# Zero products on TensorE behind two attentions and inside two layer norms, and the variances of all pairs ahead of the logits

## The reference

```python
h = jnp.concatenate([tokenise(x), txt], axis=1)                 # 8 x 269 x 64
h = h + L0_attn(_layernorm(h))       # Nystrom attention, 8 heads, 6 pseudo-inverse steps
h = h + L0_ffn(_layernorm(h))        # 8 experts, top 2, router on the normed stream
h = h + L1_attn(_layernorm(h))       # exp(-gamma * squared distance) attention, 8 heads
h = h + L1_ffn(_layernorm(h))        # shared MLP and 4 experts, top 2

def _L0_ffn_ref(x, Wr, br, ln_g, ln_b, W1, b1, W2, b2):
    logits = xt @ Wr + br
    top_p, top_idx = jax.lax.top_k(jax.nn.softmax(logits, axis=-1), TOP_K)
    ...
    xn = (xt - mu) * jax.lax.rsqrt(var + LN_EPS)
```

## Time and profile before

| what | value |
|---|---|
| median of 3 runs | 731.64 us (730.41 to 740.26) |
| the profiled execution | 736.04 us |
| its span | 734.2 us |
| mean granted clock of TensorE in it | 0.939 |
| TensorE busy | 681.5 us (93% of the span), 6033 products |
| weight loads | 527.5 us (72%) |
| VectorE, ScalarE, GpSimd busy | 413.5, 377.6 and 229.7 us |
| DMA | 8.23 MB, most of it in the first 40 us |

### The profile page before, as it was taken

The page is one execution under the profiler, slowest core; times in us unless marked ns, Lnnn a source line. Parts: engine busy times, 40 slices in busy tenths (PEclk is TensorE's granted clock), DMA queues, the critical chain, the costliest instruction groups (busy, mean ns, idle before and its releaser), DMA issues. The chain is left out here.

```text
span 734.2 us, 15178 instructions
## 1 busy us (share of the span) xinstructions
PE 681.5 (93%) x6033; PEld 527.5 (72%) x6033; DVE 413.5 (56%) x843; ACT 377.6 (51%) x1035; POOL 229.7 (31%) x204
## 2 busy tenths in 40 slices
PE   9887898999999999999889999869999999989896
PEld 5676798988989898988785555557666666647555
DVE  3457347667575767674525333426777777764322
ACT  4656447565655647473246555335555455544531
POOL 4155325343544344444300434023222222201001
PEclk9997699999999999999958999957999999996999
DMA  8200000000000000000000000000000000000000
GB/s 267 99 3 1 1 1 3 2 1 2 1 2 2 2 1 3 2 1 2 1 1 1 1 1 1 1 1 1 1 1 1 1 2 1 1 1 1 1 15 17
DMA packets 5214, 8.23 MB, mean 11 GB/s; under 512 B 3608, under 2 KB 4120, under 8 KB 4760
## 3 DMA queue, kind: packets, MB, share of 16 engines
q1 hardware_dynamic: 4552, 7.20, 3.1%
q10 hardware_dynamic: 592, 0.07, 0.1%
HBM read 6.71 MB, written 0.55 MB: 10 GB/s over the span
## 5 line engine op out<-in xcount | busy, mean ns | idle before, releaser
L977 POOL TENSOR_TENSOR STD<-STD,NN 91x492 f32<-91x492 f32 (+1 forms) x96 | 104.0, 1101 | 149.2 <-DVE NN L1106 78.7
L677 PE MATMUL PS<-ST 128*91 128x123 f32 x768 | 92.9, 272 | 4.8 <-DVE ST L1112 4.6
L1106 DVE SCALAR_TENSOR_TENSOR NN<-ST,PS 91x492 f32<-91x492 f32 x96 | 62.9, 661 | 56.3 <-PE PS L677 56.3
L677 PE MATMUL PS<-NN 128*91 128x123 f32 (+1 forms) x768 | 89.6, 268 | 3.2 <-DVE NN L1106 3.2
L677 PEld LDWEIGHTS PS<-ST 128*91 128x91 f32 x768 | 83.5, 159 | 11.0 <-DVE ST L1112 7.1
L677 PEld LDWEIGHTS PS<-NN 128*91 128x91 f32 x768 | 82.2, 160 | 10.4 <-DVE NN L1106 6.4
L1746 PE MATMUL PS<-QR,KA 128*128 128x270 f32 x256 | 72.2, 413 | 0.0
L895 ACT ACTIVATE STD<-ST 91x492 f32<-91x492 f32 (+1 forms) x96 | 51.6, 569 | 39.6 <-DVE ST L1112 39.6
L1860 DVE TENSOR_SCALAR CL<-PS,K 128x270 f32<-128x270 f32 x144 | 65.7, 496 | 9.8 <-PE PS L1746 4.5
L1112 DVE SCALAR_TENSOR_TENSOR ST<-PS,STD 91x492 f32<-91x492 f32 (+1 forms) x96 | 55.9, 599 | 22.1 <-POOL STD L977 12.4
L1801 ACT ACTIVATE EX<-CL,NG 128x540 f32<-128x540 f32 x64 | 46.7, 741 | 32.8 <-DVE CL L1860 32.7
(11 more groups left out here) (326 smaller groups left out, 1250.5 us busy)
## 6 DMA issues: line engine op xcount, KB each, us to landing
TP<-taps SPq DMA_DIRECT2D x1, 1204.0 KB, 16.1
MA<-mat SPq DMA_DIRECT2D x1, 1120.0 KB, 7.5
MF<-mat SPq DMA_DIRECT2D x1, 1024.0 KB, 12.6
WI<-wide SPq DMA_DIRECT2D x1, 902.0 KB, 9.0
CO<-const SPq DMA_DIRECT2D x1, 512.0 KB, 15.7
MQ<-mat SPq DMA_DIRECT2D x1, 512.0 KB, 16.4
out<-OS SPq DMA_DIRECT2D x8, 45.0 KB
XA<-xpatch SPq DMA_DIRECT2D x1, 256.0 KB, 2.8
```

Source lines behind the costliest of these rows:

```text
L677: last = nc.tensor.matmul(PS[0:NL, PINV + q, h % 4 * SW + c0:(h % 4 + 1) * SW], x[:, h, 0:NL], x[:, h, c0:SW], start=True, stop=True)
L977: nc.gpsimd.tensor_tensor(TD[:, 4 * q:4 * q + 4, c0:SW], SA[:, 4 * q:4 * q + 4, c0:SW], NN[0:NL, 4 * q:4 * q + 4, c0:SW], ALU.subtract).th ...
L1106: v.scalar_tensor_tensor(out=NN[0:NL, own, :], in0=ST[0:NL, b % 2, own, :], scalar=N_S, in1=heads4(PS[0:NL, PINV + q, 0:4 * SW]), op0=ALU. ...
```

## The change

ZK and spin move out of the token stage, so that all stages can use them, and spin can now also write only partitions low to 127, with 256 columns in fp32. The first attention gets two zero products ahead of its last output projection and 14 behind it, all into bank 2. The second attention gets 14 behind its last product, into bank 5, after a wait on VectorE's reads of that bank. In norm_pe the variances of all four pairs come first; then each pair has one zero product of 32 outputs (partitions 96 to 127 of bank VARS) ahead of its logits, and four such follow the last logits.

```diff
+        ZK = sb("ZK", [128, 512], F32R)
...
+        def spin(n, bank=7, low=0):
+
+            for _ in range(n):
+                if low:
+                    nc.tensor.matmul(PS[low:128, bank, 0:256], ZK[:, 0:128 - low].bitcast(F32), ZK[:, 0:256].bitcast(F32),
+                                     start=True, stop=True)
+                else:
+                    nc.tensor.matmul(PS[:, bank, :], ZK[:, 0:128], ZK[:, :], start=True, stop=True)
...
         SCORES, PROJ, PINV, TAIL = 0, 4, 4, 6
         SUMS, TOPS = 3, 1
+        SPARE = 2
...
                 attend(B - 1, 0)
                 attend(B - 1, 1)
+                spin(2, SPARE)
                 out_proj(B - 1)
+                spin(14, SPARE)
...
             for p in range(BP):
                 pe.wait_ge(sem(tag + "_squared"), p + 1)
                 variances(p, VARS, KT * p).then_inc(sem(tag + "_var"), 1)
+            for p in range(BP):
+                spin(1, VARS, 96)
                 pe.wait_ge(sem(tag + "_kept"), p + 1)
                 logits(p, weights, n).then_inc(sem(tag + "_logit"), 1)
+            spin(4, VARS, 96)
             for p in range(BP):
                 pe.wait_ge(sem(tag + "_widened"), p + 1)
...
                 batches(pe, body)
+                need(pe, ("d_vm", atb("d_vm", B // 2 - 1, 1, 4, 4)))
+                spin(14, 5)
```

More of the change, by code:

```diff
@@ L212, in program @@
         PL = ts("PL", [128, BP, NL - 1])
-        ZK = ts("ZK", [128, 512], F32R)
         HC = B * NI // 2
-        SPIN = 7
         assert HC == 256 and GRP == 3 and PAD % GRP == 1 and NI % GRP == 1 and (NX - 2) % GRP == 0
@@ L347, in _ @@
             def _(pe):
-                def spin(n):
-                    for _ in range(n):
-                        nc.tensor.matmul(PS[:, SPIN, :], ZK[:, 0:128], ZK[:, :], start=True, stop=True)
                 avp = CO[:, C_AVP:C_AVP + 128]
```

## The result

The changed kernel takes 739.51 us (median of 4 runs, 735.84 to 749.78), the kernel before 731.58 us beside it (4 runs, 730.41 to 740.26). The ratio is 1.0083, with an interval of 1.0046 to 1.0119: some 6 us longer (+3.4 to +8.7), where +0.7 was forecast. The ratio leaves out the slow one of the changed kernel's four runs, 749.78 us at a granted clock of 0.939 where the other three have 0.953 to 0.959, and so it gives a smaller difference than the two medians. The forecast's range of 725 to 742 us held the result, and it is within 2%. The profiled execution took 735.84 us with a span of 734.0 and a mean granted clock of 0.959; the one of before took 736.04 with 734.2 and 0.939. So the two profiles alone would say "no change, at a better clock", and the times say otherwise. That is the question of this study.

A forecast was written before the change was run, and what follows sets the result against it. TensorE, busy 93% of the span, was taken as the bound, its clock dipping in both norms. Held norms -3.9 us plus one fall +4.6 gave +0.7; 731.64 + 0.7 = 732.3 us, range 725 to 742.

The forecast's parts named there:

- The barriers: Behind each attention, 14 zero products make TensorE last at the barrier, delaying the centring by +2.4 and +2.5 us.
- The order in the norm with the clock held: In both norms at high clock, TensorE reaches the spreading 9.24 us after the centring's start, instead of 11.79 and 8.27.
- d: Norm before the first feed-forward, after the first attention; predicted -4.3 us with the clock held.
- h: Norm before the last feed-forward, after the second attention; predicted +0.4 us with the clock held.
- Does the clock hold: Likeliest, chance 0.40: it holds in one norm and falls in the other, a fall costing +4.6 us (+1.8 to +7.4).
- The base of the sum: Whole kernel: gains set against the profiled 736.04 us, then carried to the median, 4.4 us lower, giving 731.64.
- milestones: Gate weights' cast at 393.91 and turn at 683.50 us; work behind them was called the same and at full clock.
- B: Rival, chance 0.22: the clock falls in both norms, zero products run at half clock before the spreading; +5.3 us, 736.9.
- A: Rival, chance 0.25: the clock holds in both norms; -3.9 us, 727.7.
- C: Rival, chance 0.04: zero products with 32 outputs don't keep the clock up, low from the first logits; +14.4 us, 746.
- D: Rival, chance 0.05: the norm's zero products run beside the logits, saving 1.9 us per norm; A would be 723.9.
- The warned place: In the norm, reciprocals ready at 5.3 us, but logits and zero products cover the early variances' worth; 3.9 us slack.

The follow-up runs named there:

- e4: Changed kernel without the norms' eight zero products and with 4 instead of 14 behind each attention; 0.9906 of the kernel before, median 726.04 us.
- e1: Changed kernel with the old norm order and no zero products in the norm, keeping 2, 14 and 14 around the attentions; 1.0112 of the kernel before.
- b2: The kernel before, unaltered, profiled a third time; a single execution of 734.26 us.
- e2: Changed kernel without the zero products around the attentions, only the norm's edit kept; 1.0176 of the kernel before.
- e7: Kernel before with only the variances of all pairs moved ahead of the logits, no zero products added; 0.9943 of the kernel before.
- e10: Changed kernel with the norm's eight zero products as fp32r, 128 outputs, 512 columns, into bank 5; 1.0161 of the kernel before.
- e6: Changed kernel with the old norm order, no zero products in the norm, and 2, 4 and 4 around the attentions; 1.0029 of the kernel before.

## Why the prediction was nearly right, and where it was not

**The barriers: right.** 2.83 became 5.18 (+2.35 for +2.4 predicted), 2.47 became 4.93 (+2.46 for +2.5). The barrier did wait for TensorE's queue. The two zero products ahead of the projection cost nothing, as said: the projection starts 0.05 us behind ScalarE's copy.

**The order in the norm with the clock held: the right mechanism, one term mis-sized.** The spreading was to come 9.24 us behind the centring and came at 10.21 in both profiles of d. Of the missing 1.0 us 0.8 are in the alternation: a zero product and the logits of one pair take 0.55 (372.59 to 373.14) and 0.58 us (373.14 to 373.72) in turn, where I had 0.45 and 0.48. The rest is in the centring (1.90 for 1.80) and the last four zero products (1.85 for 1.80). Rows of one form confirm the prediction's prices, 0.46 for the last four zero products and 0.48 for e4's logits; each change between the two adds 0.1. It is not so between any two forms: in e1 variances and logits alternate at 0.48 each, as its timeline shows:

```profile
374.60 0.62 PE L1237 MATMUL PS<-CO,LSQb 128*90 128x2 f32 x6
375.08 0.63 PE L1245 MATMUL PS<-WI,LCEb 128*90 128x16 f32 x6
375.56 0.62 PE L1237 MATMUL PS<-CO,LSQb 128*90 128x2 f32 x6
```

I had priced both from rows in which they ran among their own kind.

The roots came 3.95 us behind the centring (3.8 predicted), the first reciprocals were wide at 5.35 (5.3), and from the spreading on d took 9.66 (9.64 predicted), h 10.98 (11.43).

**Does the clock hold: right in kind, by two profiles.** It held in one norm and fell in the other in both profiles, which was the likeliest case at 0.40. In the first profile it fell 3.3 us behind the first variance (I had 2.6 to 5.6). Against an h norm held up to the spreading (4.93 + 10.21 + 10.98 = 26.1) the fall cost 4.1 us in the first and 7.0 in the second; I had 4.6 with bounds of 1.8 and 7.4. The 10.98 is itself not quite a held one: its spreading took 3.64 us against 3.07 in d.

**The base of the sum: wrong, and this is the miss.** The prediction set its gains against the one profiled execution and carried the sum over to the median by the difference of 4.4 us, as if that lay in places that the change doesn't touch. The third profile of before shows a d norm 3.9 us shorter, and the sum over remainders suggests that this is the usual one. If so, 3.9 of the -4.3 us in d were not there to be gained in most executions: with b2 as the base, d goes from 24.45 to 25.05, +0.6, and h from 25.09 to 30.18, +5.1, together +5.7 us against the measured 6 (+8.7 with the changed kernel's second profile). By the prediction's own terms: 3.9 from the base, 1.0 from the norm's length, and +0.1 from h (the fall there was 0.5 cheaper, the norm's length 1.0 dearer, the rest 0.4 cheaper) make 5.0 of the 5.3 that it missed by. That the base is the cause is inferred from 3 profiles and the remainders, not shown run by run. A smaller error of the same kind: the prediction called the work behind its milestones the same and at full clock. The stretch from the d milestone to the second attention's end holds a fall at 480 us, and took between 262.9 and 265.2 us in the profiles.

**What the range was worth.** The measured interval of +3.4 to +8.7 us leaves out the forecast's +0.7. The range held the result because it had been made wide enough for two rivals (-6.6 to +10.4 us around the median), and that "no change by 2%" came true says little, since of all the kernels tried here only e2's interval reaches beyond 2%. The point forecast missed by nearly the whole effect, and that the result lies in the range is owed to the range's width and not to the sum.

**The rivals.** B's number (736.9) is nearest to the measured 737.7, but not for its reason: d held in both profiles. A fell with h. C fell as a rule, since in d the clock was 1.00 from 372.6 on with zero products of 32 outputs; but in h its picture nearly came, low from among the first logits on and the spreading 14.27 us behind the centring where C had 14.8, and e2 came near it in both norms (16.12 and 15.77). D fell: zero products in partitions 96 to 127 and logits with 90 outputs started 0.55 and 0.58 us apart, one after the other. The Trainium skill, TensorE: Matmul & The Clock Gate, section "Part 3: Packing small matmuls — row/col tiling", has small products run at once when each has its output in a strip of 32 of its own; the trace agrees for 32-wide ones. That a 90-wide product counts as three such strips was the prediction's own step, and the trace shows no overlap there.

**The warned place was named but undervalued.** The logits and zero products "cover all of it", the prediction says of what the early variances could be worth. That was the finding: the one line of e7 is worth 4.2 us by itself, and in the changed kernel eight zero products bury it.

## What to carry to other kernels

A zero product that keeps the clock up is free only where the engine would have stood idle: count how many fit until the slowest engine reaches the barrier (four here, not fourteen), and put none between a result that is ready and the product that wants it, since there they cost their time, and twice that when the clock falls all the same (e2 against e7: 17 us). Before a sum is set against a profile, look whether the difference between its time and the median lies in the very stretch that the change touches; profile the kernel before two or three times if it can be had. And try the parts of such a change singly and in pairs: here moving one loop gave 4.2 us, four zero products at each attention perhaps 2.7 more, and all parts together lost 6.

## What the runs showed of the hardware

Alternating zero products of 32 outputs with logits of 90 cost 0.1 us at each change, on top of 0.46 and 0.48 us, though variances and logits alternate for nothing. Eight zero products of 0.244 us (fp32r, 512 columns, 128 outputs) held the clock less well than eight of 0.46 us (fp32, 256 columns, 32 outputs): it fell in both norms of e10 (one profile) and in one of the changed kernel (two profiles). It fell in the changed kernel's h norm without any idle time of TensorE in the 5.2 us before. In two kernels (e1 and e6) the clock fell in the final products, which no edit touches, for twice 6.8 us, and the last stage was 6.5 us longer in each. And executions of one and the same kernel differ by 3.9 us in one norm for no reason that I found in the trace: in all three profiles of before the centring of d runs at the low clock, and only in b2 it recovers behind it.
